# Early-fusion transformer on one core: two VectorE copies move ahead of the maximum over the last two score banks

## The reference, cut to what matters

```python
def _attn_branch(xp, w_qkv, w_proj, b_proj, keep_heads, keep_ch):
    B2, N, C = xp.shape
    hd = C // H                                   # 12 heads of 16
    qkv = (xp @ w_qkv).reshape(B2, N, 3, H, hd).transpose(2, 0, 3, 1, 4)
    ...
    a = jax.nn.softmax(jnp.einsum('bhnd,bhmd->bhnm', q, k) * scale, axis=-1)
    o = jnp.einsum('bhnm,bhmd->bhnd', a, v).transpose(0, 2, 1, 3).reshape(B2, N, C)
    o = o @ w_proj + b_proj
    ...
x = x + attn_out
```

## Time and profile before

| what | value |
|---|---|
| three runs, median (lowest to highest) | 1114.33 us (1114.12 to 1117.25) |
| the profiled execution | 1112.48 us |
| its span in the profile | 1110.8 us |
| granted TensorE clock, mean | 0.993 of full |
| TensorE busy | 1069.5 us, 96% |
| ScalarE busy | 763.2 us, 69% |
| VectorE busy | 722.5 us, 65% |
| GpSimd busy | 570.6 us, 51% |
| chain that ended last | PE 88%, DVE 6%, ACT 3%, POOL 1% |

### The profile page before, as it was taken

How to read it: one execution, slowest core, us unless ns; L and a number is a source line. 1 busy time by engine, 2 the same in 40 slices (tenths; PEclk the granted TensorE clock), 3 DMA queues, 4 the chain that set the end, 5 groups by cost and what they waited for, 6 DMA issues and landing times.

```text
span 1110.8 us, 34055 instructions
## 1 busy us (share of the span) xinstructions
PE 1069.5 (96%) x13103; PEld 868.9 (78%) x13103; DVE 722.5 (65%) x2256; ACT 763.2 (69%) x3370; POOL 570.6 (51%) x859
## 2 busy tenths in 40 slices
PE   6999998999999999999999999999999999999998
PEld 4788886777777465358888888888888888888577
DVE  8666566666766214367887878888888878877201
ACT  2356556777787435548988889888888888887231
POOL 2156666454455676436655465565465565465200
PEclk9999998999999999999999999999999999999999
DMA  8100603000000000010000000000000000000000
GB/s 273 29 5 2 135 3 79 1 2 1 2 1 1 1 1 1 1 51 2 3 3 3 2 3 3 3 3 3 3 2 3 3 3 2 3 3 3 11 22 32
DMA packets 35056, 19.66 MB, mean 18 GB/s; under 512 B 24656, under 2 KB 32336, under 8 KB 34896
## 3 DMA queue, kind: packets, MB, share of 16 engines
q1 hardware_dynamic: 34752, 17.00, 5.8%
q10 hardware_dynamic: 144, 0.49, 0.1%
HBM read 14.93 MB, written 1.77 MB: 15 GB/s over the span
## 4 chain that ended last, share of the span: by engine, by line
PE 88%; DVE 6%; ACT 3%; POOL 1%; issue 1%; DVEq 0%; POOLq 0%
PE banks L1750 8%; PE banks L1821 8%; PE banks L1758 6%; PE banks L1837 5%; PE banks L1532 5%; PE banks L1809 4%; PE banks L1856 4%; PE banks L2202 3%; PE banks L1814 3%; PE banks L2156 3%; PE banks L505 2%; PE banks L1258 2%; PE banks L1279 2%; PE banks L1861 2%; PE banks L1797 2%; PE banks L1844 2%
## 5 line engine op out<-in xcount | busy, mean ns | idle before, releaser
L2123 POOL TENSOR_TENSOR e_W<-e_W,e_RS 128x384 f32<-128x384 f32 x256 | 205.2, 827 | 233.0 <-DVE e_RS L1997 230.8
L1947 ACT ACTIVATE e_W<-banks,e_MX 128x128 f32<-128x128 f32 x768 | 270.1, 371 | 18.1 <-DVE e_MX L1983 18.1
L1947 ACT ACTIVATION_READ_ACCUMULATOR e_W<-banks,e_MX 128x1 f32 x768 | 161.2, 210 | 0.0
L1750 PE MATMUL banks<-XT,e_wqk 64*128 64x141 f32 x744 | 119.2, 295 | 0.0
L1750 PEld LDWEIGHTS banks<-XT,e_wqk 64*128 64x128 f32 x744 | 96.3, 188 | 18.1 <-issue 16.6
L1758 PE MATMUL banks<-e_wv,XT 128*128 128x192 f32 (+3 forms) x512 | 109.9, 344 | 0.6 <-DVE e_PT L2001 0.6
L1821 PE MATMUL banks<-ident,e_W 128*128 128x128 f32 x768 | 106.1, 274 | 1.1 <-POOL e_W L2123 0.8
L1506 POOL TENSOR_TENSOR f_W<-f_W,e_RS 128x423 f32<-128x423 f32 x64 | 56.3, 892 | 90.0 <-DVE e_RST L1485 79.7
L1941 ACT COPY e_PT<-banks 128x512 f32<-128x512 f32 x128 | 68.9, 588 | 40.6 <-PE banks L1821 40.3
L1983 DVE TENSOR_REDUCE e_MX<-banks 128x3 f32<-128x384 f32 x128 | 65.4, 552 | 41.4 <-PE banks L1809 41.4
L1821 PEld LDWEIGHTS banks<-ident,e_W 128*128 128x128 f32 x768 | 87.5, 143 | 2.3 <-DVE e_V L2010 1.0
(11 more groups left out here) (328 smaller groups left out, 2724.2 us busy)
## 6 DMA issues: line engine op xcount, KB each, us to landing
xp<-in_patches_dram SPq DMA_DIRECT2D x4, 768.0 KB, 9.2
H<-in_h_dram SPq DMA_DIRECT2D x1, 1728.0 KB, 13.2
out_dram<-H SPq DMA_DIRECT2D x6, 288.0 KB, 2.3
m_hid<-in_e_gu_dram SPq DMA_DIRECT2D x1, 1536.0 KB, 9.2
m_hid<-in_e_o_dram SPq DMA_DIRECT2D x4, 192.0 KB, 6.9
e_wqk<-in_e_qk_dram SPq DMA_DIRECT2D x8, 96.0 KB, 2.5
e_wqk<-in_e_qk_dram SPq DMA_DIRECT2D x24, 32.0 KB, 2.3
tokw<-in_tok_w_dram SPq DMA_DIRECT2D x1, 576.0 KB, 5.2
```

The costliest lines, as they stand in the source:

```text
L1750: return nc.tensor.matmul(bank[6][:, m * SEQ:(m + 1) * SEQ], ew[n % EXPERTS][0][0:rows_c, c, m * P:(m + 1) * P], XT[0:rows_c, c, tokens(n) ...
L1947: ex = nc.scalar.activation(W[n % 2][:, t, :], bank[i][:, x * P:(x + 1) * P], ACT.Exp, bias=MX[:, t:t + 1], accum_out=SM[n % 2][:, t:t + 1])
L2123: nc.gpsimd.tensor_tensor(x, x, RS[n % 2][:, 3 * i:3 * i + 3].unsqueeze(2).broadcast_to([P, 3, P]), ALU.mult).then_inc(s_nm, 1)
```

## The change

The maximum over banks 2 and 3 leaves `maxima(n)` and becomes a function of its own, which is called after the copies of sets 2 and 3. No instruction is added or taken away, and no wait.

```diff
@@ -1432,6 +1432,8 @@
                         nc.vector.tensor_reduce(MXT[0:NTR, :], bank[7][0:NTR, 0:2 * SEQ].rearrange("p (i k) -> p i k", i=2),
                                                 AX.X, ALU.max, negate=True).then_inc(sf_mx, 1)
                         maximum(1)
+
+                    def last_maxima():
                         nc.vector.tensor_reduce(MX[:, 6:12].rearrange("p (i x) -> p i x", i=2),
                                                 pair23[:, :, 0:S3].rearrange("p i (x k) -> p i x k", x=3), AX.X, ALU.max,
                                                 negate=True).then_inc(sf_mx, 1)
@@ -1480,6 +1482,7 @@
                             evacuate_weights(n - 1, 2)
                             evacuate_weights(n - 1, 3)
                         if n < B:
+                            last_maxima()
                             evacuate_v(n)
                             reciprocals(n, 0, 6, 3)
                             nc.vector.reciprocal(RST[n % 2][0:NTR, :], SMT[n % 2][0:NTR, :]).then_inc(sf_rc, 1)
```

## The result

The changed kernel took 1103.24 us (median of 4 runs, 1101.58 to 1106.07), the kernel before 1114.55 (4 runs, 1114.12 to 1117.25). The ratio is 0.9896 with a 95% interval of 0.987 to 0.9922: faster, by 11.3 us or 1.0%.

The account below looks back on a forecast made before the run. TensorE, busy 96% of the span, was taken as the bound, with ScalarE limiting the gain mid-round; 15 rounds x 0.45 = 6.75 us off 1114.33 gave 1107.6 us, range 1103.8 to 1110.6.

Parts of the forecast that it names:

- Bound and prize: Elastic attention: TensorE bounds; its waits before set 4 (0.51 us) and the tail's transposes (0.16) are the whole prize.
- VectorE's part: Copies of sets 2 and 3 start without waiting; the later maximum ends 1.5 us before its reader: cost zero.
- ScalarE decides what is kept: Set 4's copy stands behind bank 1's exponentials on ScalarE, so 0.45 us a round is gained: 12.21 becomes 11.76.
- The sum of 15 rounds: Rounds n = 1 to 15 of the elastic attention each gain 0.45 us, 6.75 us in all.
- carried the difference over: Timed median lies 1.85 us above the profiled execution; kept for the changed kernel: 1114.33 - 6.75 = 1107.6 us.
- Rival one: TensorE's fall to half clock in round 1 stays away: 2.9 us on top, 9.6 in all, 1104.7 us; 10%.
- Two: ScalarE already bounds mid-round and set 4's copy starts no earlier: no gain that can be told, 1112 to 1114 us; 9%.
- Three: VectorE idles before the copies, waiting for TensorE's sets 2 and 3: at 1.6 us wait, 9.9 us slower, 1124.2; 3%.

Follow-up runs that it names:

- after_again: The changed kernel run again with no edit, beside the kernel before: 1101.60 us median of 6 runs, ratio 0.9919.
- before_filled: The kernel before plus 20 matmuls whose result nobody reads, in TensorE's idle stretches of rounds 0 and 1: 1114.25 us.
- v_copy_ahead: The kernel before with VectorE's copy of V also ahead of its copies of sets 2 and 3: 1129.79 us, ratio 1.0161.

## Why the prediction was right, and where it failed

- **Bound and prize.** Right: TensorE's two waits, not the length of the maximum. One bank of the maximum in front cost nothing.
- **VectorE's part.** Right, cost zero: no idle time before the copies, the last maximum 1.48 us ahead of its reader (1.5 forecast).
- **ScalarE decides what is kept.** Right: 0.45 us a round, the wait of 0.48 before the tail, rounds of 11.76. Moving ScalarE's copy gave a further 0.25 a round; giving TensorE other work for that wait gave 0.28.
- **The sum of 15 rounds.** 6.75 was forecast; the fastest runs, at a mean clock of 0.997 or 0.998, lie 6.3 us apart, in two sessions. The rounds themselves give the full 0.45 each, round 1 too: from round 0's scores (L1244) to the first tail it is 14.40 us before and 13.95 after. The 0.4 us that are missing are no more than the few tenths by which the start of the phase differs between profiles (these scores start at 167.36 and 167.41 us in two profiles of the kernel before, at 167.71, 167.32 and 167.74 in three of the changed one).
- **The step that failed** is the one that carried the difference over: "The timed runs have a median 1.85 us above that execution, and I carry the difference over: 1114.33 - 6.75". It took the base for a fixed number, and so both kernels for equally far from their full speed. The 4 runs of before in that session all lay 6.7 to 9.8 us above the fastest run of this kernel (1107.45), and the changed kernel's median 2.1 us above its own (1101.15): 6.3 + 7.1 - 2.1 = 11.3. Rival one named the mechanism, but gave it 10%, one place and 2.9 us, and the lower end of the range was set by it. Its price for round 1 was right: tail 1 to tail 2 is 14.59 us before and 11.14 in after_again, which has full clock there, 3.0 more than the order's 0.45. But there are more places. The trace of before shows the start of the expert phase near 497 us too, which the prediction doesn't name, and the profiles of the other versions show stretches near 39, 169, 339, 398 and 414 us. In the profiled pair the 9.2 us of span are 6.75 from the rounds, 1.6 from round 1's clock (tail 1 to tail 2: 14.59 against 12.55 us, less 0.45), 1.3 from the clock at 497 us, less 0.4 at the start of the phase. What stays open is why that session's base was so high: in the later sessions only 9 of 55 runs of the kernel before took 1114 us or more, in the first all 4 did, which is hardly chance from run to run alone.
- **Rivals.** Two fell with the rounds of 11.76. Three fell, and its price was confirmed: 0.90 us of delay, 0.90 us a round.
- **Does the new order also spare the clock?** The trend says so: in the two later sessions that had both kernels the mean is 1110.3 us for before (44 runs), 2.8 above its fastest, and 1101.9 for the changed kernel (11 runs), 0.7 above its own. That is 2.1 us beyond the order. The half clock at the start of the expert phase stands in all four profiles of kernels with VectorE's old order (two of the kernel before, before_filled, and v_copy_ahead, where it comes at 513 us) and in none of the nine with the new one.

These two lines of TensorE's timeline, of the kernel before and of the changed kernel, are the same eight transposes behind the same wait:

```profile
496.99 1.81 PE L1821 MATMUL banks<-ident,e_W 128*128 128x128 f32 x8 [0.79 <-POOL e_W L2123]
489.02 1.35 PE L1824 MATMUL banks<-ident,e_W 128*128 128x128 f32 x8 [0.79 <-POOL e_W L2126]
```

From there to the product that next waits for VectorE (0.60 us in both) it is 5.62 us before and 4.36 after, the 1.3 of the sum above. So the idle time just ahead doesn't decide whether the clock falls there. What does is open: the four start these transposes at 496.99 us or later, the nine at 493.76 or earlier, and no run separated the order from such a shift in time.

The Trainium skill (TensorE: Matmul & The Clock Gate, section "What's actually happening") has the clock follow recent activity, watched on a count that does not start anew with the kernel, so that the same kernel can meet it at another place from run to run. The levels of one kernel from 1107.5 to 1117.2 us with mean clocks from 0.998 to 0.989 agree with that. This does not say by itself why the clock fell at the expert phase in all four profiles with the old order and in none of the nine with the new one.

## What to carry to other kernels

What a move off the chain is worth is read from the idle time of the bounding engine and from who is next in line, engine by engine; a timeline drawn from start-to-start distances gave the new order's round here to 0.01 us, while those drawn for three of the experiments missed by 0.05 to 0.11 us a round. The base of the sum needs the same care: with three runs of a kernel whose clock has levels, ask on which level they and the profiled run stand, list every stretch of the trace at the lower clock with its price, and let the range hold all of them coming or going.

## What was not expected of the hardware

- The same program had times from 1107.5 to 1117.2 us on one core, by stretches in which TensorE was granted half its clock: 1.9 to 3.7 us above the fastest at a mean clock of 0.996, 6.7 or 6.8 at 0.992, 9.4 to 9.7 at 0.989.
- Such a stretch can turn a gain round: the projection moved ahead saved 2.5 us over 12 rounds, and the median did not fall, because the two rounds behind them idled longer and, in the profiled run, ran partly at half clock.
- ScalarE begins a copy 0.09 us after the start of a read of the sum, though that read is on record for 0.24 us.
